# GNN and expert kernel on one core: weight loads issued later at two places, and five filler matmuls after the first experts

## The reference, cut to what matters

```python
x = x + gnn0(layernorm(x), edges)     # 3 diffusion steps over a 256x256 adjacency
x = x + ffn(layernorm(x))             # 8 experts 512 -> 1024 -> 512, each token takes its best 2
x = x + gnn1(layernorm(x), edges, edge_attr)
x = x + lstm_moe(layernorm(x))        # 8 experts, one LSTM step each, best 2

def gnn1(h):                          # 4352 edges
    m   = relu(concat(h[src], edge_attr) @ W1.T + b1) @ W2.T + b2
    agg = segment_sum(m, dst)
    gi, gh = agg @ W_ih.T + b_ih, h @ W_hh.T + b_hh
    r, z = sigmoid(gi_r + gh_r), sigmoid(gi_z + gh_z)
    n = tanh(gi_n + r * gh_n)
    return h + batchnorm((1 - z) * n + z * h)
```

## Time and profile before

| what | value |
|---|---|
| median of 3 runs (lowest, highest) | 451.18 us (449.94, 453.32) |
| the profiled execution's own time | 453.09 us |
| its span, first to last instruction | 451.2 us |
| granted clock of TensorE over the span | 0.987 of full |
| busy: PE, DVE, ACT, POOL | 420.7, 388.8, 296.1, 132.0 us |
| bytes moved by DMA | 116.20 MB, mean 258 GB/s |

### The profile page before, as it was taken

The page is one execution under the profiler, slowest core; times in us unless marked ns, Lnnn a source line. Parts: engine busy times, 40 slices in busy tenths (PEclk is TensorE's granted clock), DMA queues, the critical chain, the costliest instruction groups (busy, mean ns, idle before and its releaser), DMA issues.

```text
span 451.2 us, 6292 instructions
## 1 busy us (share of the span) xinstructions
PE 420.7 (93%) x2252; PEld 344.5 (76%) x2252; DVE 388.8 (86%) x628; ACT 296.1 (66%) x349; POOL 132.0 (29%) x141
## 2 busy tenths in 40 slices
PE   4999999999999995897999999999999999998994
PEld 2776788888888784676889998867778777886883
DVE  6988899988889868588899985969999988999693
ACT  7975477877786752633444455559788788877552
POOL 7984110111100032148678500032112323000400
PEclk9999999999999998799999999999999999999999
DMA  7933498899899846796766405327988999989711
GB/s 235 341 106 97 143 366 316 306 373 393 347 370 333 338 167 241 278 371 214 214 193 233 143 20 191 115 100 271 355 313 322 382 350 365 381 298 356 264 50 49
DMA packets 26213, 116.20 MB, mean 258 GB/s; under 512 B 7084, under 2 KB 8268, under 8 KB 15296
## 3 DMA queue, kind: packets, MB, share of 16 engines
q1 hardware_dynamic: 18672, 93.78, 56.0%
q0 software_dynamic: 7216, 21.79, 15.0%
q10 hardware_dynamic: 288, 0.15, 0.1%
HBM read 109.15 MB, written 6.55 MB: 256 GB/s over the span
## 4 chain that ended last, share of the span: by engine, by line
PE 65%; DVE 17%; POOL 4%; DMA 4%; issue 4%; ACT 3%; SPq 1%; DVEq 0%; ACTq 0%; POOLq 0%
PE bank L1735 13%; PE bank L1742 12%; PE bank L1736 12%; DVE wlo L1062 6%; PE bank L2215 4%; PE bank L2217 3%; PE bank L1728 3%; PE bank L1727 2%; PE bank L1726 2%; PE bank L2098 2%; PE bank L2022 2%; DVE wlo L1067 2%; DMA node_rows<-A_sb 2%; DMA gath<-node_rows,src_i 1%; PE bank L1751 1%
## 5 line engine op out<-in xcount | busy, mean ns | idle before, releaser
L1062 DVE TENSOR_TENSOR wlo<-raw,whi 128x2048 fp32r<-128x2048 f32 x69 | 156.0, 2285 | 12.1 <-ACT whi L723 12.0
L723 ACT ACTIVATE whi<-raw 128x2048 fp32r<-128x2048 f32 x73 | 138.0, 1915 | 7.5 <-PE bank L2184 5.4
L1735 PE MATMUL bank<-whi,xe_hi 128*128 128x512 f32 (+1 forms) x200 | 78.0, 393 | 1.1 <-ACT xe_hi L756 0.7
L1736 PE MATMUL bank<-wlo,xe_hi 128*128 128x512 f32 (+1 forms) x200 | 76.0, 383 | 0.0
L665 POOL DMA_INDIRECT xg<-node_rows,idx x14 | 26.1, 1864 | 129.3 <-DVE idx L1360 129.3
L1742 PE MATMUL bank<-whi,xe_lo 128*128 128x512 f32 (+1 forms) x200 | 51.9, 381 | 0.2 <-DVE xe_lo L1353 0.2
L699 POOL DMA_INDIRECT gath<-node_rows,src_i x34 | 42.6, 1253 | 17.5 <-DVE mp L1646 8.1
L1735 PE MATMUL bank<-whi,hT_hi 128*128 128x512 f32 (+1 forms) x124 | 46.9, 385 | 0.7 <-ACT hT_hi L786 0.4
L1736 PE MATMUL bank<-wlo,hT_hi 128*128 128x512 f32 (+1 forms) x124 | 45.0, 369 | 0.0
L1735 PEld LDWEIGHTS bank<-whi,xe_hi 128*128 128x128 f32 x200 | 37.6, 188 | 9.1 <-ACT xe_hi L756 0.9
L1736 PEld LDWEIGHTS bank<-wlo,xe_hi 128*128 128x128 f32 x200 | 37.7, 188 | 7.1
(11 more groups left out here) (327 smaller groups left out, 884.7 us busy)
## 6 DMA issues: line engine op xcount, KB each, us to landing
raw<-in_weights_dram SPq DMA_DIRECT2D x85, 1024.0 KB, 6.5
y_rows<-y_sb POOLq DMA_DIRECT2D x16, 256.0 KB, 6.2
ea<-in_ea_dram SPq DMA_DIRECT2D x8, 256.0 KB
node_rows<-xn POOLq DMA_DIRECT2D x4, 256.0 KB, 2.4
gath<-node_rows,src_i POOLq DMA_INDIRECT x34
x<-in_x_dram SPq DMA_DIRECT2D x1, 512.0 KB, 3.8
gw<-in_L_ffn_gw_dram SPq DMA_DIRECT2D x1, 512.0 KB, 9.3
node_rows<-A_sb POOLq DMA_DIRECT2D x2, 256.0 KB, 7.4
```

Of the source, the lines that this page charges most:

```text
L723: act.activation(whi[n % SPL][:, :, :], raw[n % RAW][:, :, :], ACT.Copy).then_inc(hi_cut, 1)
L1062: dve.tensor_tensor(wlo[n % SPL][:, :, :], raw[n % RAW][:, :, :], whi[n % SPL][:, :, :].bitcast(f32), ALU.subtract).then_inc(lo_cut, 1)
L1735: pe.matmul(ps, xh[:, blocks + k, :], whi[w % SPL][:, k, cs], start=first and k == 0, stop=False)
L1736: pe.matmul(ps, xh[:, blocks + k, :], wlo[w % SPL][:, k, cs], start=False, stop=False)
```

## The change

It touches two programs, SP's and PE's.

1. SP, end of the first experts: Whh0 and Whh2 are issued as before. Whh1 now waits until PE has transposed tile 0 (`xt_ps >= 5`), and W2 is moved behind the first three loads of edge attributes, where Wih0 stood.
2. SP, edge stage: Wih0, Wih1 and Wih2 are moved behind the edge attributes of groups 5, 6 and 7. A load of group g (g of 3 or more) waits for the cuts of group g-2, which happen once every four tiles of the stage.
3. PE: five fillers into bank 7 stand in front of the transposes of tile 0.

```diff
             for n in range(NT):
                 sp.wait_ge(y_in[n], 16 * 2)
             jobs_cut(ffn, number, EC)
-            main(GNN_ORDER[1:5])
+            main(GNN_ORDER[1:3])
+            sp.wait_ge(xt_ps, 2 * NT + 1)
+            main(GNN_ORDER[3:4])
             sp.wait_ge(xt_sb, 2 * NT + 2)
             for g in range(3):
                 edge_attr(g)
-            main(GNN_ORDER[5:8])
+            main(GNN_ORDER[4:5])
             for g in range(3, NG):
                 edge_attr(g)
+                if g >= NG - 4 and g < NG - 1:
+                    main(GNN_ORDER[g + 9 - NG:g + 10 - NG])
             main(LSTM_ORDER)
...
             experts(ffn)
 
 
+            keep_busy(B[7], 5)
             turn_x(2, (0,))
             keep_busy(B[0], 2)
```

## The result

| kernel | median of 22 runs (lowest, highest) | ratio to before, with its 95% interval |
|---|---|---|
| before | 452.74 us (449.94, 455.17) | 1 |
| changed | 454.06 us (450.76, 456.68) | 1.0038 [1.0021, 1.0055] |

The change costs 0.4%, some 1.7 us, with an interval that leaves out no change and every gain. The forecast was 1.7 us in the other direction. Its 449.5 us started from a median of 451.18 over three runs; over 22 that median is 452.74, so 1.6 of the 4.6 us between 449.5 and the measured 454.06 lie in the starting value and not in the change.

What follows compares the result with a forecast made beforehand. PE bounds the kernel, slowed by half clock at 175 to 187 us and DMA waits at 199 to 208. 1.9 - 0.2 - 0 = 1.7 us gained: 451.18 to 449.5 us, own range 448.5 to 451, full range 446.4 to 452.0.

Steps and rivals of the forecast that it cites:

- I take 196, since its last part runs alone: Second store of A_sb, issued at 191.71, lands at 196 us, between bounds of 194.1 and 199.4.
- rival (a): Store of A_sb: W2 holds it until 199.4, gather again needs over 5 us, gain 0, 451.4 us; chance 0.13.
- rule of turns among the queues: DMA engines alternate among queues, so any chunk under way delays the A_sb store; W2 alone would hold it as Wih0 did.
- I take 0 for all three: Edge stage: Wih0 to Wih2 among the gathers cost 0; bounds 0 and 3 x 2.6 us.
- everything behind the first sum hangs on it and slides with it: From the edge stage's first sum on, all later work moves earlier by the forecast 1.7 us.
- even a store that lands at 199.4 gives a gather at 203.1, if the queue is empty by then: First gather of the edge stage: still lands before the edge product is done at 204.1, despite a late store.
- rival (c): Edge stage: the three chunks starve the gathers, up to 2.6 us each, 6.1 us lost, 457.3 us; chance 0.06.
- Rows 12: Profile rows cited for the edge stage: in 232 to 238 us PE is busy 6.00 of 6.00 us at 262 GB/s.
- -0.2: End of first experts: with the fillers PE reaches tile 1's transposes at 186.5, 0.2 us later; bounds 0.8 gained, 1.7 lost.
- B: Time PE goes on after its second stop near tile 0's transposes: 183.69 before, 182.2 forecast, bounds 181.15 and 183.69.
- (d): PE's second stop: instruction block comes no sooner, at 183.69, 1.7 us lost instead of 0.2, 451.0 us; chance 0.13.
- The 1.9 at the first sum: First sum of the edge stage starts at 206.4 instead of 208.34, 1.9 us gained; bounds 0 and 2.0.

Runs made afterwards that it cites:

- e9: Kernel before with ten fillers instead of fifteen ahead of the first gating (34 us), loads as before: 448.81 us, ratio 0.9920.
- e2: Kernel before with only Whh1 and W2 held back, Wih0 to Wih2 following W2 at once, no fillers added: 453.42 us, ratio 1.0036.
- e18: Full change, five fillers included, with W2 released together with Whh1, ahead of the first edge attributes: 452.32 us, ratio 0.9997 of before.
- e3: Full change without its five fillers, so both load edits on the kernel before: 453.28 us, ratio 1.0023 of before.
- e10: e9 with both load edits of the change and no fillers ahead of the transposes: 451.48 us, ratio 0.9977 of before.
- e11: e9 with the full change on top, its five fillers included: 452.07 us, ratio 0.9995 of before.
- e1: Kernel before with only Wih0 to Wih2 moved among the gathers, no hold, no fillers added: 451.93 us, ratio 1.0001.
- e15: e9 with only the move of Wih0 to Wih2 among the gathers: 448.34 us, ratio 0.9905 of before.
- e4: Kernel before with only the five fillers ahead of tile 0's transposes, loads as before: 453.58 us, ratio 1.0040.
- e13: e9 with Wih0 to Wih2 moved behind all edge attributes: 450.89 us, ratio 0.9950 of before.
- e5: Kernel before with five fillers in a pause at 6.3 us, none at the first experts' end, loads as before: 453.80 us, ratio 1.0028.
- e6: Kernel before with nine fillers in the pause at 6.3 us, loads as before: 455.87 us, ratio 1.0064.
- e14: e9 with only the hold of Whh1 and W2, Wih0 to Wih2 behind W2: 452.11 us, ratio 0.9984 of before.
- e12: Kernel before, unchanged, run again for a second profile: store of A_sb 6.8 us, stage 53.2 us; no median given.

## Why the prediction was wrong

**Edit 1, "I take 196, since its last part runs alone": this step failed.** The second store landed 6.6 and 7.0 us after its issue in the two profiles, where the forecast had 4.3 (196 less 191.71); so far it was rival (a), which had 0.13. Less data behind W2 did not help; the one chunk beside the store did all of the harm (median 6.6 to 7.8 us in the kernels that have a load there, and 2.8 to 3.6 in the six that have none; e9's 4.9 is a first store of 3.8, out before Wih0, and a second of 6.1 beside it). The gain of edit 1 by itself is nil (e2), and the 3 us store comes from edit 2, which clears Wih0 to Wih2 away, provided that W2 is not put in their place. The Trainium skill's rule of turns among the queues (DMA: Bandwidth & Descriptors, "Queues, rings and completion order"), which the forecast had weighed against itself, is what these stores agree with: with any chunk under way the second one takes 6.1 to 7.7 us, with none 2.3 to 3.1.

**Edit 2, "I take 0 for all three", and "everything behind the first sum hangs on it and slides with it": this step failed too, and it cost the time.** The stage did not slide, it grew: 57.5 and 56.2 us from first to last sum, where it was 54.9 and 53.2. With W2 ahead of the stores and nothing else moved it is 54.2, and the kernel 1.9 us faster (e18). So the three chunks cost nothing that the runs can tell behind a quick store, and some 2 to 3 us of the stage behind a slow one.

**The price of rival (a) was wrong as well.** It had the gather need over 5 us behind a slow store; it needed 3.7 to 3.8 (e3, e10, e11), as the forecast had allowed for ("even a store that lands at 199.4 gives a gather at 203.1, if the queue is empty by then"). I let a late store cost the gain and nothing else, and gave starved gathers their own rival (c), on the ground that gathers run five tiles ahead. Rows 12 show that lead late in the stage. At its start there is none until the gathers have had time to outrun the sums, and the late store takes that time. So (a) brought a part of (c) with it: 1.1 to 3.0 us of waiting, some 2 us of the stage. The move of the chunks by itself was rightly put at 0: 0.0 in e1, -0.15% in e15 against e9, both within the noise. In e1 the 0 is partly luck, 1.4 us gained at the first sum and some of it lost to the wait at 219.86.

**Edit 3, "-0.2", bounds +0.8 and -1.7.** The mechanism was right in most steps: fillers behind the branch at half clock, the stop bound to the program and now right behind the transposes. B was sized well enough in the change (4.8 and 4.7 us behind the branch, against 4.6 forecast), as the hold makes it earlier (4.4 to 5.2 us behind the branch in four profiles, though 5.9 in e11). But the transposes came 1.2 and 1.7 us later by the mark, not 1.0, since the branch was 0.4 and 0.8 us later. With four chunks under way the fillers cost 1.8 us alone (e4), the size of (d)'s 1.7; beside the load edits their 0.7 us (e3) are within the noise. The clock, put back at the same place as before, came back 4.7 us earlier by the mark in the first profile (184.5) and 1.3 us later in the second (187.9).

**The sum.** 1.9 - 0.2 - 0 was forecast. Measured, each edit alone: hold -1.6, fillers -1.8, move 0; all together -1.7, so they do not add up. The 1.9 at the first sum did come (0.6 to 3.2 us in the two profiles), by the edge product ending the wait, just as forecast; it was then lost 10 us later in the stage.

## What to carry to other kernels

Where a store must land before indirect reads can begin, keep every large load off the queues for its 3 us, even one: it took twice as long beside a single 1 MB chunk, and the reads behind it lost the lead that hid most of the later loads. Behind a conditional block, ask where in the engine's program the next stop falls: five fillers (ten instructions) fewer, 140 us further up and in a pause, moved it behind useful work and gave 0.8%, more than any edit to the loads. Before a gain of 1% is read out of one profile, take a second: the two of each kernel here differ by 1.3 and 1.7 us in the edge stage.

## What was not expected of the hardware

- The stop behind the branch mostly ends 5.7 to 6.2 us after it with four chunks (4 MB) under way (7.0 in e13), and after 4.4 to 5.2 us with the hold as the change has it (5.9 in e11), wherever the program stands then. It is not worth the same everywhere: 1.55 us of pause (before), 3.64 (e5), 6.15 on the branch itself (e6), none in e9 but 1.31 in e13.
- Adding ten or 18 instructions in a pause near the start of the program, where they delay nothing, cost 1.3 and 2.9 us; taking ten away gained 3.6.
- What stays open: the hold alone lost 1.6 us (e2) while its profile, of an execution well below its median, has no late first sum; e14 shows such a loss, e2 does not. How the 1.8 us of e4 arise, and why an mp of e1 waits for its gather with the lead there, is open too. In the first profile of the changed kernel the waits at 218.9 are put down to PE's sums and not to gathers; why PE's signals came late there was not settled. The longer loads in the LSTM experts (in the first profile of the change, in e3 and in e12, so in kernels with and without the change) were not looked into.
